# Two local transformers in a hybrid network: 32-query blocks of 64 keys, a mask added in the scores' bank, values on the streaming side, a skewed stream

## The reference, cut to what matters

```python
def local_attention(q, k, v):            # windows of 32 tokens, each sees itself and the one before
    bq, bk, bv = blocks of 32
    bk2, bv2 = (look(bk), look(bv))      # 64 keys: the last window and this one
    mask = (it < jb) | (it > jb + w) | (jb == -1)
    sim = jnp.einsum('bhwie,bhwje->bhwij', bq, bk2) * QK_SCALE
    sim = jnp.where(mask, -jnp.finfo(sim.dtype).max, sim)
    return jnp.einsum('bhwij,bhwje->bhwie', jax.nn.softmax(sim, -1), bv2)

# attn_layer: q, k, v = x @ Wqkv; q, k = l2norm, scale, rotary; out = local_attention @ Wo
# ffn_layer:  layernorm, a * gelu(gate) of width 341, @ W2 + b2
```

## Time and profile before

| | us |
|---|---|
| median of 3 runs | 4346.1 |
| lowest and highest run | 4344.21, 4350.79 |
| the profiled execution | 4339.8 span |
| PE busy | 3995.2 (92%) |
| DVE busy | 3715.0 (86%) |
| ACT busy | 3380.3 (78%) |
| POOL busy | 3380.2 (78%) |

### The profile page before, as it was taken

One profiled execution on the slowest core, in us unless ns is written; L12 is line 12 of the kernel. 1 busy time (PEld: TensorE's weight loads), 2 busy tenths in 40 slices (PEclk: granted clock), 3 DMA queues, 4 the chain that ended last, 5 costly groups with the idle time before them and its releaser, 6 DMA issues. The chain is left out here.

```text
span 4339.8 us, 130231 instructions
## 1 busy us (share of the span) xinstructions
PE 3995.2 (92%) x46283; PEld 2655.5 (61%) x46283; DVE 3715.0 (86%) x12505; ACT 3380.3 (78%) x10657; POOL 3380.2 (78%) x4196
## 2 busy tenths in 40 slices
PE   6888799999999999999767999999999999996686
PEld 2333357767767767766553677767776776763464
DVE  6999789999999999999476999999999999974646
ACT  5888489999999999999414999999999999983122
POOL 3999698888888888888296888888888888861313
PEclk7999899999999999999897999999999999997887
DMA  1000101111111111111002111111111111100000
GB/s 28 1 1 1 46 24 31 41 31 36 41 27 49 31 34 44 26 34 27 15 1 53 31 27 41 36 41 31 36 41 27 51 29 29 37 24 3 6 3 10
DMA packets 78571, 122.04 MB, mean 28 GB/s; under 512 B 26024, under 2 KB 47204, under 8 KB 77924
## 3 DMA queue, kind: packets, MB, share of 16 engines
q1 hardware_dynamic: 77924, 113.71, 10.3%
HBM read 35.56 MB, written 1.05 MB: 8 GB/s over the span
## 5 line engine op out<-in xcount | busy, mean ns | idle before, releaser
L1095 POOL TENSOR_TENSOR local_qk<-local_qk,local_rb 128x512 f32<-128x512 f32 x768 | 975.7, 1271 | 224.2 <-DVE local_rb L1485 210.1
L1365 ACT ACTIVATE local_pr<-local_tb,local_nmax 128x96 f32<-128x96 f32 x3072 | 995.0, 362 | 68.7 <-DVE local_nmax L1501 67.1
L1191 PE MATMUL local_pj<-local_wqkv,local_xs 128*128 128x512 f32 x1536 | 808.4, 619 | 31.8 <-DVE local_rb L1485 17.8
L1101 POOL TENSOR_TENSOR local_qk<-local_qk,local_rinv 128x512 f32<-128x512 f32 x768 | 786.6, 1045 | 7.5
L1501 DVE CUSTOM_DVE_ANT_0 local_tb<-local_tb,local_mask 128x96 f32<-128x96 f32 x3072 | 689.2, 290 | 46.5 <-PE local_tb L1213 43.7
L1365 ACT ACTIVATION_READ_ACCUMULATOR local_pr<-local_tb,local_nmax 128x1 f32 x3072 | 703.3, 229 | 0.0
L1117 POOL TENSOR_TENSOR local_pr<-local_pr,local_rsum 128x384 f32<-128x384 f32 x768 | 622.4, 826 | 36.5 <-DVE local_rsum L1507 36.5
L1482 DVE TENSOR_TENSOR local_qk<-local_pj,local_rope 128x512 f32<-128x512 f32 x768 | 523.6, 682 | 62.8 <-ACT local_sq L1348 44.1
L1348 ACT ACTIVATE local_sq<-local_pj 128x512 f32<-128x512 f32 x768 | 462.2, 627 | 123.3 <-PE local_pj L1191 119.0
L1485 DVE TENSOR_TENSOR local_rb<-local_pj,local_rope 128x512 f32<-128x512 f32 x768 | 523.2, 681 | 2.8 <-POOL local_qk L1095 2.8
L1492 DVE TENSOR_REDUCE local_ss<-local_sq 128x8 f32<-128x512 f32 x768 | 512.0, 678 | 2.6 <-ACT local_sq L1348 0.8
(11 more groups left out here) (425 smaller groups left out, 7954.8 us busy)
## 6 DMA issues: line engine op xcount, KB each, us to landing
local_v<-local_v SPq DMA_DIRECT2D x288, 256.0 KB, 3.9
local_wqkv<-L_ffn_Wqkv_dram SPq DMA_DIRECT2D x72, 256.0 KB, 4.7
local_wo<-L_ffn_Wo_dram SPq DMA_DIRECT2D x12, 512.0 KB, 4.0
local_w<-L_ffn_W_dram SPq DMA_DIRECT2D x12, 341.0 KB, 4.8
mamba_parts<-mamba_in_low SPq DMA_DIRECT2D x24, 64.0 KB, 2.0
local_w<-L_ffn_W_dram SPq DMA_DIRECT2D x12, 128.0 KB
y_dram<-store_xtok SPq DMA_DIRECT2D x4, 256.0 KB, 2.9
local_oT<-rope_dram SPq DMA_DIRECT2D x2, 256.0 KB, 2.7
```

The lines of the kernel that those rows point to most:

```text
L1095: nc.gpsimd.tensor_tensor(qk[:, u, :], qk[:, u, :], rb[:, u % 2, :], ALU.add).then_inc(s["summed"], 1)
L1101: nc.gpsimd.tensor_tensor(heads8(qk[:, u, :]), heads8(qk[:, u, :]), r, ALU.mult).then_inc(s["scaled"], 1)
L1191: nc.tensor.matmul(bank[:, :], xs[:, par, u // 4 * P:(u // 4 + 1) * P], wqkv[:, dep % 2, u % 4 * BANK:(u % 4 + 1) * BANK], start=True, sto ...
L1365: ins = nc.scalar.activation(pr[:, (NU * c + k) % PR_RING, i, WIN:WIN + KW], scores[:, i * KW:(i + 1) * KW], ACT.Exp, scale=-1.0, bias=nma ...
```

## The change

Blocks become 32 queries (`QB = 32`) with 64 keys (`KW = 64`), and pieces go by tiles of 128 tokens (`TILES = 2`). A score piece is now 64 matmuls of 32 queries by 64 keys, on eight tiles of the array of 64 rows by 32 columns; there are two of them. `maxima` has 4 pieces: one addition of a bfloat16 mask to a whole bank in place, a wait for it, and one reduction of the bank to 8 maxima with the sign turned. `exps` has 4 pieces of 8. The probabilities are turned without being scaled. In `weigh` (2 pieces of 64 matmuls) they are now the stationary side and v streams by, so the output comes with tokens on the partitions; VectorE's `scale_o` divides it by the sums, a new `turn_o` (2 pieces of 16 transposes) turns it, and ScalarE's `copy_o` writes `oT`. `norm_p` is gone.

v is held for each block in the partitions that it needs, through eight transfers per item (`move_v`, `window`). The stream itself is stored skewed: the upper 64 channels stand one token later, so the shifted input needs no copy, `shift_in` and the second residual are gone, and output and down projection write 257 columns, each half of the channels by a matmul of its own. The layer norm's inverse root is taken by GpSimd as two more columns of the root of q and k, three items later (`ROOT_LEAD`), and `spread_root` makes its diagonal; `std` and `spread_std` are gone. b2 is a row of `w2`. A second bank `fa` takes the place of `ob`. The lists of steps, lags and turns of banks are new on all engines; TAIL is 5.

```diff
-QB = 64
+QK_COUPLES = QK_UNITS // 2
+
+
+QB = 32
 KW = QB + WIN
+HALF = P // 2
+BLOCKS = P // QB
 PAIRS = HEADS // 2
-COUPLES = 4
-NU = 2 * COUPLES
-PR_RING = 6
-PT_RING = 2
+TILES = L // P
...
+                need(sp, s["pv_ready"], TILES * (b - 1))
+                moved = s[f"v_moved{b % 2}"]
+                for h in range(2):
+                    row, other = h * HALF, (1 - h) * HALF
+                    sp.dma_start(vw[row + QB:row + 2 * QB, par, 4:6, :, :], v[0:QB, par, :, h, :, :]).then_inc(moved, 16)
+                    sp.dma_start(vw[row:row + HALF, par, 0:2, :, :], v[other:other + HALF, par, :, h, :, :]).then_inc(moved, 16)
+                    sp.dma_start(vw[row:row + HALF, par, 2:4, :, :], v[QB:3 * QB, par, :, h, :, :]).then_inc(moved, 16)
+                    sp.dma_start(vw[row:row + QB, par, 5, :, :], v[3 * QB:P, par, 0, h, :, :]).then_inc(moved, 16)
...
+            def spread_root(e, par, _):
+                pool.wait_ge(s["root_steps"], ROOT_ALL * (e + ROOT_LEAD + 1))
+                pool.wait_ge(s["var_ready"], e + 1)
+                nc.gpsimd.tensor_tensor(work[:, :].rearrange("p (t c) -> p t c", t=TILES), view(net.ident[:, :], [[0, TILES], [1, P]]),
+                                        view(rinv[:, 2 * 2 * HEADS:NR], [[1, TILES], [0, P]]), ALU.mult).then_inc(s["diag_ready"], 1)
...
+            def score(c, par, t):
+
+                sc = free_pair("score", c, t)
+                if t == 0 and c == 0:
                     pe.wait_ge(s["pad_ok"], 1)
-                if kk % 2 == 0:
-                    pe.wait_ge(s["qk_copied"], QK_UNITS * c + 4 * t + 4)
-                for i in range(4):
-                    for h, low in ((0, 0), (1, 1), (0, 1), (1, 0)):
-                        own, p, q = slice(h * DH, (h + 1) * DH), 4 * half + i, QB * (2 * t + low)
-                        ins = nc.tensor.matmul(sc[h][low * QB:(low + 1) * QB, i * KW:(i + 1) * KW], qT[own, par, p, q:q + QB],
-                                               kT[own, par, p, q:q + KW], start=True, stop=True)
+                pe.wait_ge(s["qk_copied"], QK_UNITS * c + 4 * t + 4)
+                for p in range(PAIRS):
+                    for i in range(BLOCKS):
+                        for h in range(2):
+                            own, q = slice(h * DH, (h + 1) * DH), t * P + i * QB
+                            ins = nc.tensor.matmul(sc[h][i * QB:(i + 1) * QB, p * KW:(p + 1) * KW], qT[own, par, p, q:q + QB],
+                                                   kT[own, par, p, q:q + KW], start=True, stop=True)
                 ins.then_inc(s["scored"], 1)
 
-            def turn_probs(c, par, kk):
-                banks = free_pair("probs", c, kk)
-                pe.wait_ge(s["weighted"], NU * c + 2 * kk + 2)
-                for h in range(2):
-                    for i in range(4):
-                        for low in range(2):
-                            rows, at = slice(low * QB, (low + 1) * QB), (4 * h + i) * QB
-                            ins = nc.tensor.transpose(banks[low][:, at:at + QB], pr[rows, (NU * c + 2 * kk + h) % PR_RING, i, :], net.ident[rows, rows])
+            def turn_probs(c, par, t):
+                banks = free_pair("probs", c, t)
+                pe.wait_ge(s["exped"], 4 * c + 2 * t + 2)
+                for p in range(PAIRS):
+                    for low in range(2):
+                        rows = slice(low * HALF, (low + 1) * HALF)
+                        ins = nc.tensor.transpose(banks[low][:, p * HALF:(p + 1) * HALF],
+                                                  pr[rows, (TILES * c + t) % PR_RING, p, :, :].rearrange("q h k -> q (h k)"), net.ident[rows, rows])
                 ins.then_inc(s["probs_turned"], 1)
...
+            def weigh(c, par, t):
+
+                ob = free_pair("weigh", c, t)
+                pe.wait_ge(s["probs_copied"], 4 * c + 2 * t + 2)
+                if t == 0:
+                    pe.wait_ge(s[f"v_moved{c % 2}"], MOVES * (c // 2) + MOVES)
+                for p in range(PAIRS):
+                    for i in range(BLOCKS):
+                        for h in range(2):
+                            at = p * HALF + i % 2 * QB
+                            ins = nc.tensor.matmul(ob[h][i * QB:(i + 1) * QB, p * DH:(p + 1) * DH], prT[h * KW:(h + 1) * KW, t, i // 2, at:at + QB],
+                                                   window(par, BLOCKS * t + i, h)[:, p, :], start=True, stop=True)
+                ins.then_inc(s["pv_ready"], 1)
+
+            def turn_o(c, par, t):
+                banks = free_pair("o", c, t)
+                pe.wait_ge(s["o_scaled"], 4 * c + 2 * t + 2)
+                for p in range(PAIRS):
                     for low in range(2):
-                        for h in range(2):
-                            ins = nc.tensor.matmul(ob[h * DH:(h + 1) * DH, i * P + low * QB:i * P + (low + 1) * QB],
-                                                   v[:, par, V_BLOCK[2 * t + low], 2 * (4 * half + i) + h, :],
-                                                   prT[:, kk % PT_RING, low, (4 * h + i) * QB:(4 * h + i + 1) * QB], start=True, stop=True)
-                ins.then_inc(s["pv_ready"], 1)
+                        rows = slice(low * HALF, (low + 1) * HALF)
+                        ins = nc.tensor.transpose(banks[low][:, p * HALF:(p + 1) * HALF],
+                                                  o[rows, t, p, :, :].rearrange("q h k -> q (h k)"), net.ident[rows, rows])
+                ins.then_inc(s["o_turned"], 1)
...
                 for j in range(4 * part, 4 * part + 4):
-                    ins = nc.tensor.matmul(fb[:, 0:L], wo[:, j, :], oT[:, j, :], start=(j == 0), stop=(j == INNER // P - 1))
+                    for h in range(2):
+                        own = slice(h * HALF, (h + 1) * HALF)
+                        ins = nc.tensor.matmul(fa[own, 0:L + 1], wo[:, j, own], oT[:, j, 1 - h:L + 2 - h], start=(j == 0), stop=(j == INNER // P - 1),
+                                               skip_group_check=True)
...
             def iteration(run):
+                run(spread, 5, 0)
+                run(turn_probs, 3, 1)
+                run(turn_qk, 2, 0)
...
+                t, h = divmod(k, 2)
+                act.wait_ge(s["maxed"], 4 * c + k + 1)
+                need(act, s["probs_turned"], TILES * c + t - PR_RING + 1)
+                need(act, s["sum_inv"], TILES * (c - 1) + t + 1)
+                scores = pair_of_banks("score", t)[h]
+                for p in range(PAIRS):
+                    ins = nc.scalar.activation(pr[:, (TILES * c + t) % PR_RING, p, h, :], scores[:, p * KW:(p + 1) * KW], ACT.Exp,
+                                               bias=nmax[:, t, h, p:p + 1], accum_out=esum[:, t, h, p:p + 1])
                 ins.then_inc(s["exped"], 1)
...
+            def copy_o(c, par, k):
+                t, low = divmod(k, 2)
+                act.wait_ge(s["o_turned"], TILES * c + t + 1)
+                if k == 0:
+                    need(act, s["wo_ready"], c)
+                    if c == 0:
+                        act.wait_ge(s["oT_ok"], 1)
+                at = 1 + t * P + low * HALF
+                nc.scalar.activation(oT[:, :, at:at + HALF], heads8(pair_of_banks("o", t)[low][:, :]), ACT.Copy).then_inc(s["o_copied"], 1)
...
+                t, h = divmod(k, 2)
+                dve.wait_ge(s["scored"], TILES * c + t + 1)
+                need(dve, s["exped"], 4 * (c - 1) + k + 1)
...
+                scores = pair_of_banks("score", t)[h][:, :].rearrange("p (a k) -> p a k", k=KW)
+                nc.vector.tensor_tensor(scores, scores, view(maskb[:, t, 0:1], [[0, PAIRS], [1, KW]]), ALU.add).then_inc(s["masked"], 1)
+                dve.wait_ge(s["masked"], 4 * c + k + 1)
+                nc.vector.tensor_reduce(nmax[:, t, h, :], scores, AX.X, ALU.max, negate=True).then_inc(s["maxed"], 1)
+
+            def recip(c, par, t):
+                dve.wait_ge(s["exped"], 4 * c + 2 * t + 2)
+                nc.vector.reciprocal(rsum[:, t, :, :], esum[:, t, :, :]).then_inc(s["sum_inv"], 1)
+
+            def scale_o(c, par, k):
+
+                t, h = divmod(k, 2)
+                dve.wait_ge(s["pv_ready"], TILES * c + t + 1)
+                dve.wait_ge(s["sum_inv"], TILES * c + t + 1)
+                need(dve, s["o_turned"], TILES * (c - 1) + t + 1)
+                nc.vector.tensor_tensor(o[:, t, :, h, :], heads8(pair_of_banks("weigh", t)[h][:, :]),
+                                        view(rsum[:, t, h, 0:1], [[1, PAIRS], [0, DH]]), ALU.mult).then_inc(s["o_scaled"], 1)
...
+                nc.vector.tensor_tensor(z1[:, par, :], stream[:, e % B, 0:L + 1], fa[:, 0:L + 1], ALU.add).then_inc(s["z1_ready"], 1)
...
+                need(dve, s["root_steps"], ROOT_ALL * (e + ROOT_LEAD - 1))
+                nc.vector.tensor_scalar(normx[:, (e + ROOT_LEAD) % 2, 2 * 2 * HEADS:], fb[:, L:L + TILES], LN_EPS, None, ALU.add).then_inc(s["var_in"], 1)
```

607 lines of the change are left out of this document (249 added, 358 removed).

## The result

The changed kernel takes **4589.4 us**, median of 4 runs (4580.7 to 4594.7), against 4345.2 for the kernel before: a ratio of 1.056, 95% interval 1.054 to 1.058. It is 5.6% slower. I had forecast 4205 and a range up to 4320, so the sign is wrong, and the size by 380 us. The profiled execution has a span of 4583.4 us.

A forecast was written before the change was run, and what follows sets the result against it. TensorE's work bounds the kernel; after the change 23.7 us of it plus a 7.4 us chain make 31.2 an iteration instead of 32.7. Times 96 that is 144 us less, 4 more for normalisation: 4205 us, range 4115 to 4320.

The forecast's parts named there:

- What bounds the kernel now: In the two local transformers' plateaus TensorE never waits; its own work is the iteration, other engines have 2 to 4 us slack.
- the iteration of 32.7 us: Length of one iteration before the change, from the starts of the layer norm's spread: 19 iterations, 18 gaps.
- TensorE's list: Sum of TensorE's unit costs in an iteration, forecast at 29.2 us after the change.
- The weigh unit's 1.08 us for each new unit: Four new score and weigh units at 1.08 us each, 4.3 us instead of 7.6: 3.3 us less an iteration.
- rival 2: Score and weigh units bound by 25.6 ns a record: 3.3 us a unit, iteration 37.8, kernel 4835 us; chance 4%.
- A rule that speaks against it: The skill's floor of about 25 ns between matmul starts, by which a new unit of 128 records would take 3.2 us.
- Changes of shape, 0.7 us: Eight changes of tile shape on TensorE between the transposes and the last score unit, 0.7 us of the 23.7.
- The chain from the scores to the transposes, 7.4 us, and a wait of 2.0: Last score unit through mask, reduction and exponentials takes 7.4 us; TensorE has 5.4 of work there, so waits 2.0.
- If that were all: Without a new wait from the changed order, an iteration would be 29.2 us.
- The rivals: Other outcomes: eight tiles not overlapping 12%, pace of records 4%, more waits 16%, TensorE's list alone or partly 7%.
- rival 1: Eight tiles do not overlap as four do: score and weigh units 2.0 us, iteration 34.0, kernel 4470 us; chance 12%.
- What would show it: Expected signs: units about 1.1 us, iterations 31.2, one 2 us wait before probabilities' transposes, TensorE busy near 94%, VectorE 80%.

The follow-up runs named there:

- a bad and a good place: Changed kernel with 31 transposes an iteration done twice, block borders placed by once-only copies of one transpose: 120 or 80 copies 4662.6 and 4660.3 us, 64 copies 4558.9 us.
- the good one: Changed kernel with 31 transposes of each iteration done twice and 64 copies of one transpose in the first stage to place the block borders: 4558.9 us.

## Why the prediction was wrong

- *What bounds the kernel now, the iteration of 32.7 us, TensorE's list*: right. So were VectorE, ScalarE and GpSimd: none of them came near to binding, and their savings were worth nothing.
- *The weigh unit's 1.08 us for each new unit*: wrong, 1.41. This is the term from which the rest of the error grows. I reasoned per tile: 512 columns for each tile, now as then. True, but I kept the columns of a tile and left out the count of instructions, which went from 32 records a unit to 128. By columns a unit would be 1.08; half the columns still cost 1.22, half the records (in bfloat16) 0.61. Four units make 1.3 us an iteration, and the one ahead of the spread takes 1.6, another 0.2. My rival 2 was of the right kind, a pace of records, but I took the only pace that rows showed, 25.6 ns, as its price, and gave it 4%. The pace is 9.5 to 11 ns.
- *A rule that speaks against it*: the Trainium skill, "TensorE: Matmul & The Clock Gate", section "Wait — 56ns, not 53.3ns?", says that matmuls never start less than about 25 ns apart, however few columns they have. For matmuls on eight tiles the trace disagrees: 11 ns on the mean of a unit.
- *Changes of shape, 0.7 us*: 1.3. The cut of the units and transposes has put a change of tile between nearly all of the twelve projections. They take 11.65 us, where twelve at 0.86 are 10.3; before they took 11.06.
- *The chain from the scores to the transposes, 7.4 us, and a wait of 2.0*: the mechanism was right, the place too, the size nearly: 8.0 us (1213.86 to 1221.89) and 1.6. The rows above show its steps: 1.51 instead of 1.20 to VectorE's start, since the unit is longer; 1.55 instead of 1.46 from there to the first exponential, ahead of which ScalarE copies a part of v; 4.62 for the exponentials (4.6 forecast); and 0.35 instead of 0.1 from ScalarE's next instruction to the transposes.
- *If that were all*: list 31.4 and wait 1.6 are 33.0. An iteration without a hole (873.6 to 906.6 us) has 33.1. Already this is slower than before: the list was to shrink by 3.5 us and shrank by 1.2, and the new wait takes more than that.
- *No term for the supply of instructions*: the step that is missing. The holes are 1.3 us. The clock at its lower level is 0.5 more; 18 of its 22 falls in the 89 iterations come within 4 us of a hole, but most holes have no fall behind them, and so the holes' part in it is likely and not shown. The profile before had what was needed: the page's list of queues has q8 with 370 transfers of 16 KB, 94712 instructions of TensorE divided by 256, about one in 12 us; the first six rows, a dense stretch, have 134 records and as many weight loads in 6.1 us, and in full iterations no 256 instructions in a row last under 5.4 us. The new unit has 128 records and 128 weight loads in 1.4. The Trainium skill, "Runtime: NRT & Kernel Launch", section "Instruction fetch mechanics", says that instructions come in blocks of 16 KB, 256 instructions each, and that crossing from one to the next is mostly hidden. The trace agrees on the blocks (147416 instructions in 575 transfers) and disagrees on "hidden" (holes of up to 2.3 us, 1.3 us an iteration).
- *The rivals*: none was what happened. The time lies between rival 1's 4470 and rival 2's 4835, by another way than either. From 31.2 to 35.0 are 3.8 us: the list 2.2 longer, holes 1.3, clock 0.5, other waits 0.3, the forecast wait 0.9 shorter on the mean, and the 0.4 that the ways of measuring leave. List and wait alone are enough for the sign, since an iteration without a hole is 0.4 us longer than before; the holes and the clock, 1.8 us, are most of the size.
- *What would show it*: TensorE's busy share from 1200 to 1600 us is 93% (371.1 of 400 us), near to the 94% forecast, but by luck: the iteration is longer, and holes stand where only the wait was to be. VectorE's is 74%, not 80. The share says little; the list of waits says it.

## What to carry to other kernels

A tile of half the size needs twice the instructions for the same columns, and TensorE's time for many small matmuls is a count of records and weight loads (here 9.5 to 11 ns for a pair) before it is a count of columns. Look at how long 256 instructions last in the densest stretch: of the block borders inside score and weigh units of the changed kernel that came less than 3 us behind the border before, 34 of 42 had a hole of over 0.3 us; of those more than 5 us behind it, 6 of 171. Put sparse work (wide projections) between dense units, or use one pass instead of two, before thinning out other engines. Cutting the units won back 42 of the 244 us here, bfloat16 in all of them 314.

A gain of 1.2 us on the engine that binds is easily lost to one wait that the new order makes. If the dense work cannot be thinned, the place of the borders can be chosen: 2% lay between a bad and a good place here, 0.7% between the changed kernel and the good one.
